# Attention over tokens on one Trainium2 core: the late scores and the late products taken by pairs of images instead of by fours

## The reference

```python
x = x + _L0_conv_ref(_gn(x), ...)       # deformable attention, 16 keys an image
t = _to_tokens(x)                       # 8 images, 256 tokens, 32 channels
t = t + _L1_attn_ref(_ln_t(t))          # below
t = t + _L1_ffn_ref(_ln_t(t), ...)      # 16 experts, each takes its 8 best tokens of an image

def _L1_attn_ref(inputs):
    scores = jnp.einsum('bqd,bkd->bqk', inputs, inputs)
    weights = jax.nn.softmax(scores, axis=-1)
    return jnp.einsum('bqk,bkd->bqd', weights, inputs)
```

## Time and profile before

| | before |
|---|---|
| median of 3 runs | 58.74 us |
| the profiled execution | 58.65 us |
| its span | 56.5 us |
| TensorE busy, share of the span | 48.0 us, 85% |
| VectorE busy | 38.7 us |
| ScalarE busy | 29.3 us |
| granted clock of TensorE | 0.999 |

### The profile page before, as it was taken

How to read it: one execution, slowest core, us unless ns; L and a number is a source line. 1 busy time by engine, 2 the same in 40 slices (tenths; PEclk the granted TensorE clock), 3 DMA queues, 4 the chain that set the end, 5 groups by cost and what they waited for, 6 DMA issues and landing times.

```text
span 56.5 us, 1445 instructions
## 1 busy us (share of the span) xinstructions
PE 48.0 (85%) x568; PEld 38.6 (68%) x568; DVE 38.7 (68%) x102; ACT 29.3 (52%) x68; POOL 20.2 (36%) x48
## 2 busy tenths in 40 slices
PE   3996997799699888999989947979999998979910
PEld 3994795687378776889867925655788585968600
DVE  2459399881849999959998475658368866685440
ACT  0813032696999396004865465297964839801000
POOL 6116389857678889960071040300000000000000
PEclk9999999999999999999999999999999999999999
DMA  0699941110000000000000000000000000000013
GB/s 0 158 194 274 240 158 46 59 46 22 0 0 0 0 0 12 6 0 0 0 0 0 0 0 6 0 0 12 0 0 0 0 0 0 12 0 0 0 49 137
DMA packets 3926, 2.02 MB, mean 36 GB/s; under 512 B 2640, under 2 KB 3792, under 8 KB 3920
## 3 DMA queue, kind: packets, MB, share of 16 engines
q1 hardware_dynamic: 1424, 1.37, 8.8%
q10 hardware_dynamic: 2496, 0.57, 4.7%
HBM read 1.68 MB, written 0.26 MB: 34 GB/s over the span
## 4 chain that ended last, share of the span: by engine, by line
PE 44%; DVE 19%; POOL 15%; ACT 7%; issue 5%; DMA 5%; DVEq 0%; ACTq 0%; POOLq 0%
DMA x_sb<-x_rows 5%; PE ps L711 4%; PE ps L792 4%; PE ps L917 3%; PE ps L858 3%; PE ps L900 3%; PE ps L804 3%; DVE taps L1100 3%; PE ps L922 2%; POOL w_smp L504 2%; ACT e_tok L654 2%; POOL d_prob L412 2%; PE ps L721 2%; DVE off L1102 2%; PE ps L747 2%
## 5 line engine op out<-in xcount | busy, mean ns | idle before, releaser
L711 PE MATMUL ps<-zeros 128*128 128x128 bf16 x128 | 10.8, 246 | 1.0 <-DVE zeros L1081 1.0
L711 PEld LDWEIGHTS ps<-zeros 128*128 128x128 bf16 x128 | 9.5, 113 | 1.5 <-DVE zeros L1081 1.0
L538 ACT ACT_TABLE_LOAD x4 | 5.1, 1283 | 1.7 <-PEq L1326 1.7
L654 ACT ACTIVATE e_tok<-ps,cst 128x512 f32<-128x512 f32 (+1 forms) x6 | 4.5, 828 | 1.5 <-PE ps L900 1.5
L1131 DVE COPY_PREDICATED ps<-over,ps 128x608 f32<-128x608 uint32 (+1 forms) x4 | 3.1, 776 | 0.7 <-PE ps L764 0.7
L453 POOL TENSOR_TENSOR wblk<-wts,cst 128x256 f32<-128x256 f32 x4 | 2.5, 625 | 2.4 <-DMA wts<-weights 2.4
L764 PE MATMUL ps<-rpe_blk,minus_hat_rel 128*32 128x168 f32 x64 | 2.8, 316 | 0.5 <-DVE minus_hat_rel L1127 0.5
L764 PEld LDWEIGHTS ps<-rpe_blk,minus_hat_rel 128*32 128x32 f32 x64 | 2.0, 141 | 1.3 <-issue 0.9
L527 POOL TENSOR_TENSOR x_tok<-ln_c 128x256 f32<-128x256 f32 x2 | 1.2, 617 | 4.7 <-ACT ln_c L639 4.7
L917 PE MATMUL ps<-e_tok,t 128*32 128x128 f32 (+1 forms) x48 | 2.8, 310 | 0.0
L900 PE MATMUL ps<-t_t 32*128 32x256 f32 x32 | 2.3, 398 | 0.4 <-ACT e_tok L654 0.4
(11 more groups left out here) (184 smaller groups left out, 126.8 us busy)
## 6 DMA issues: line engine op xcount, KB each, us to landing
w_sb<-weight ACTq DMA_DIRECT2D x1, 256.0 KB, 6.3
w_sb<-weight SPq DMA_DIRECT2D x1, 256.0 KB, 4.9
x_nat<-x_rows SPq DMA_DIRECT2D x8, 32.0 KB
wts<-weights SPq DMA_DIRECT2D x1, 192.5 KB, 3.9
cst<-shape_consts SPq DMA_DIRECT2D x1, 192.0 KB, 3.5
cst<-shape_consts SPq DMA_DIRECT2D x1, 130.0 KB, 4.8
x_sb<-x_rows SPq DMA_DIRECT2D x1, 128.0 KB, 2.7
x_sb<-x_rows ACTq DMA_DIRECT2D x1, 128.0 KB, 2.8
```

The source lines that it names most:

```text
L538: nc.scalar.add_instruction(mybir.InstLoadActFuncSet(name=nc.get_next_instruction_name(), act_func_set_id=functions, ins=[], outs=[]))
L654: return nc.scalar.activation(dst, scores, ACT.Exp, bias=const("bound"))
L711: mm(bank(n_bank, P), zeros[:, :], zeros[:, :], start=True, stop=True)
```

## The change

Five things are changed together.

1. The second half of tokens is normalised, turned and copied in two pieces, images 0 to 3 and images 4 to 7, each with 128 columns. The pieces are turned into two banks, 7 and 0. The first scores wait for the first piece alone.
2. The turn of the second half of the centred tokens stands behind the scores of images 0 to 3.
3. The scores of the late images are made in two pairs: images 4 and 5 (into banks 4 and 5) after the first exponential, images 6 and 7 (into banks 2 and 3) after the second, with the turn of `x_tok` between them. The banks of the first pair of early images are swapped with it. The fourth exponential now covers images 4 and 5 whole, the last two images 6 and 7 by query half.
4. GpSimd folds images 0 and 1, VectorE images 2 and 3.
5. The products of early and late images go by pair: first both token halves of one pair, then both of the other.

```diff
-        t1t_ps = [bank(6 + h, NT * P).rearrange("p (t m) -> p t m", t=NT) for h in range(NHALF)]
+        t1t_ps = bank(6, NT * P).rearrange("p (t m) -> p t m", t=NT)
+        t1t_late_ps = [bank(n, P) for n in (7, 0)]
-        first_banks, second_banks = [(2, 3), (4, 5)], (6, 7)
-        late_ps = ps[:, 1024:3072].rearrange("p (b h q) -> p b h q", b=B4, h=NHALF)
+        first_banks, second_banks = [(4, 5), (2, 3)], (6, 7)
+        late_ps = [ps[:, 512 * a:512 * a + 1024].rearrange("p (b h q) -> p b h q", b=2, h=NHALF) for a, _ in first_banks]
...
+            pool.wait_ge(exp_ready, NHALF)
+            fold(nc.gpsimd, 0).then_inc(folded_ready, 1)
...
-            act.wait_ge(t1_ready, NHALF)
+            act.wait_ge(t1_ready, 1 + NT)
             keep_centred(1)
...
             act.wait_ge(scores_done, 4)
-            exponent(e_tok[:, B4:, 0], late_ps[:, :, 0]).then_inc(exp_ready, 1)
+            exponent(e_tok[:, B4:B4 + 2], late_ps[0]).then_inc(exp_ready, 1)
+            act.wait_ge(scores_done, 5)
             for q in range(NHALF):
                 queries = slice(P * q, P * q + P)
-                exponent(e_tok[:, B4:, 1, queries], late_ps[:, :, 1, queries]).then_inc(exp_ready, 1)
+                exponent(e_tok[:, B4 + 2:, :, queries], late_ps[1][:, :, :, queries]).then_inc(exp_ready, 1)
...
             keep_busy("t1_second", 5)
-            turn_t1(1)
-            pe.wait_ge(ln_c_ready, 2)
-            turn_half(ct_ps, ln_c, 1).then_inc(c_turned, 1)
+            for t in range(NT):
+                pe.wait_ge(t1_ready, 2 + t)
+                turn_t1(t1t_late_ps[t], 1, t).then_inc(t1_turned, 1)
...
             score_first(0).then_inc(scores_done, 1)
             score_second(0)
+            pe.wait_ge(ln_c_ready, 2)
             score_first(1).then_inc(scores_done, 1)
             score_second(1).then_inc(scores_done, 1)
+            turn_half(ct_ps, ln_c, 1).then_inc(c_turned, 1)
+            pe.wait_ge(t1_copied[1], NT)
+            def score_late(n):
+
+                pe.wait_ge(exp_ready, n + 1)
+                for h in range(NHALF):
+                    for b in range(2):
+                        last = score(late_ps[n][:, b, h], B4 + 2 * n + b, h, start=(h == 0))
+                return last
+
+            score_late(0).then_inc(scores_done, 1)
             for h in range(NHALF):
                 pe.wait_ge(x_tok_ready, h + 1)
                 last = turn_half(conv_ps, x_tok, h)
             last.then_inc(conv_done, 1)
 
+            score_late(1).then_inc(scores_done, 1)
+
             pe.wait_ge(ones_set, 1)
             pe.wait_ge(c_copied, NT)
-            pe.wait_ge(exp_ready, NHALF)
-            for h in range(NHALF):
-                for b in range(B4, B):
-                    last = score(late_ps[:, b - B4, h], b, h, start=(h == 0))
-            last.then_inc(scores_done, 1)
-
-            pe.wait_ge(exp_ready, NHALF + 1)
-            for h in range(NHALF):
-                for b in range(B4):
-                    last = attend(early_ot_ps, b, h, slice(0, M), start=(h == 0), stop=(h == 1))
+            for n in range(2):
+                pe.wait_ge(exp_ready, NHALF + n)
+                for h in range(NHALF):
+                    for b in range(2 * n, 2 * n + 2):
+                        last = attend(early_ot_ps, b, h, slice(0, M), start=(h == 0), stop=(h == 1))
             last.then_inc(ot_done, 1)
...
+            def add_up_late(n, q):
+
+                for h in range(NHALF):
+                    for b in range(B4 + 2 * n, B4 + 2 * n + 2):
+                        last = add_up(late_sums_ps[:, q], b, e_tok[:, b, h, P * q:P * q + P], start=(h == 0), stop=(h == 1))
+                return last
+
+            def attend_late(n, q):
+
+                for h in range(NHALF):
+                    for b in range(B4 + 2 * n, B4 + 2 * n + 2):
+                        last = attend(late_ot_ps[q], b, h, slice(P * q, P * q + P), start=(q == 1 and h == 0), stop=(h == 1))
+                return last
+
             for q in range(NHALF):
-                queries = slice(P * q, P * q + P)
-                for b in range(B4, B):
-                    add_up(late_sums_ps[:, q], b, e_tok[:, b, 0, queries], start=True, stop=False)
-                for b in range(B4, B):
-                    attend(late_ot_ps[q], b, 0, queries, start=(q == 1), stop=False)
+                add_up_late(0, q)
+                attend_late(0, q)
             for q in range(NHALF):
-                queries = slice(P * q, P * q + P)
                 pe.wait_ge(exp_ready, NHALF + 2 + q + 1)
-                for b in range(B4, B):
-                    last = add_up(late_sums_ps[:, q], b, e_tok[:, b, 1, queries], start=False, stop=True)
-                last.then_inc(sums_done, 1)
-                for b in range(B4, B):
-                    last = attend(late_ot_ps[q], b, 1, queries, start=False, stop=True)
-                last.then_inc(ot_done, 1)
+                add_up_late(1, q).then_inc(sums_done, 1)
+                attend_late(1, q).then_inc(ot_done, 1)
...
+            for t in range(NT):
+                images = slice(B4 * t, B4 * t + B4)
+                tt(t1[:, 1, images], centred_ps(1)[:, t],
+                   ln_rstd[:, 0, 1, images].unsqueeze(2).to_broadcast([P, B4, C]), ALU.mult).then_inc(t1_ready, 1)
+
+            for t in range(NT):
+                dve.wait_ge(t1_turned, 2 + t)
+                nc.vector.tensor_copy(t1_t[:, t, P:], t1t_late_ps[t]).then_inc(t1_copied[1], 1)
...
-            for n in range(2):
-                images = slice(2 * n, 2 * n + 2)
-                dve.wait_ge(exp_ready, NHALF + n)
-                tt(e_fold[:, images], e_tok[:, images, 0], e_tok[:, images, 1], ALU.add).then_inc(folded_ready, 1)
+            dve.wait_ge(exp_ready, NHALF + 1)
+            fold(nc.vector, 1).then_inc(folded_ready, 1)
```

More of the change, by code:

```diff
@@ L413, in by_denominator, with fold @@
                                         ALU.mult)
+        def fold(engine, n):
+            images = slice(2 * n, 2 * n + 2)
+            return engine.tensor_tensor(e_fold[:, images], e_tok[:, images, 0], e_tok[:, images, 1], ALU.add)
         @block.sync
@@ L647, in _ @@
             act.wait_ge(t1_turned, 1)
-            nc.scalar.activation(t1_t[:, :, 0:P], t1t_ps[0], ACT.Copy).then_inc(t1_copied[0], 1)
-            act.wait_ge(t1_ready, NHALF)
+            nc.scalar.activation(t1_t[:, :, 0:P], t1t_ps, ACT.Copy).then_inc(t1_copied[0], 1)
+            act.wait_ge(t1_ready, 1 + NT)
             keep_centred(1)
@@ L879, in turn_half, with turn_t1 @@
                 return last
[L881 to L886, removed]
+            def turn_t1(out, h, t):
+                return nc.tensor.transpose(out, t1_rows[:, h, P * t:P * t + P], ident)
             pe.wait_ge(ln_c_ready, 1)
@@ L890, in _ @@
             keep_busy("t1_ready", 5)
-            turn_t1(0)
+            pe.wait_ge(t1_ready, 1)
+            for t in range(NT):
+                last = turn_t1(t1t_ps[:, t], 0, t)
+            last.then_inc(t1_turned, 1)
             keep_busy("t1_second", 5)
-            turn_t1(1)
-            pe.wait_ge(ln_c_ready, 2)
-            turn_half(ct_ps, ln_c, 1).then_inc(c_turned, 1)
+            for t in range(NT):
+                pe.wait_ge(t1_ready, 2 + t)
+                turn_t1(t1t_late_ps[t], 1, t).then_inc(t1_turned, 1)
             def score(scores, b, h, start=True):
@@ L1190, in _ @@
             dve.wait_ge(ln_c_ready, 1)
[L1191 to L1198, removed]
+            dve.wait_ge(ln_rstd_ready, 1)
+            tt(t1[:, 0].rearrange("p (t b) c -> p t b c", t=NT), by_image(ln_c[:, 0]), by_token(ln_rstd[:, 0, 0]),
+               ALU.mult).then_inc(t1_ready, 1)
+            dve.wait_ge(ln_rstd_ready, 2)
+            for t in range(NT):
+                images = slice(B4 * t, B4 * t + B4)
+                tt(t1[:, 1, images], centred_ps(1)[:, t],
+                   ln_rstd[:, 0, 1, images].unsqueeze(2).to_broadcast([P, B4, C]), ALU.mult).then_inc(t1_ready, 1)
+            for t in range(NT):
+                dve.wait_ge(t1_turned, 2 + t)
+                nc.vector.tensor_copy(t1_t[:, t, P:], t1t_late_ps[t]).then_inc(t1_copied[1], 1)
             dve.wait_ge(c_turned, 1)
```

## The result

The changed kernel takes 60.25 us (median of 6 runs, 60.13 to 60.55); the kernel before, run beside it, 58.88 (median of 6). Two of the six executions of the kernel before, 59.99 and 60.38 us, are slow ones, and the ratio leaves them out: it is 1.0263, with an interval of 1.0218 to 1.0308. The profiled execution took 60.14 us with a span of 58.1 us, against 58.65 and 56.5.

The account below looks back on a forecast made before the run. TensorE's queue was taken to bound the kernel; 0.68 + 0 + 1.54 - 0.25 = +1.97 on the profiled 58.65 us gave 60.6 us. The forecast's own range was 60.1 to 61.0, the 8-in-10 range 59.0 to 61.1.

Parts of the forecast that it names:

- Tokens in two pieces: Start of the first scores: 35.18 instead of 35.58 us, -0.40 (bounds -0.25 and -0.50).
- Up to the first product: TensorE from early scores to first product: four scores in two groups cost what eight did, products start at 39.48, +0.68.
- Exponentials and folds at nothing: ScalarE's exponentials and the folds on GpSimd and VectorE: their waits are covered, so they cost nothing.
- Early products by pair: Products of images 0 to 3: three rounds instead of two, sums sharing the third, late products after three as now: 0.
- Late products by pair: Late sums and products: images 6 and 7 begin with the eighth round of 4 and 5, +1.54 (bounds 0 and 1.76).
- starts in program order: TensorE's queue: a matmul doesn't start before the one ahead of it has started; the late products' 1.54 follows this rule.
- a queue that is one matmul deep: Variant for the late products: gains one round, 60.4 us, inside the forecast's range; no chance of its own.
- Behind them: Squares after the late products: query halves end further apart, the 0.22 us wait goes, -0.25 (bounds 0 and -0.35).
- the chances for a change within 2%: Verdict odds: 0.20 from the full-overlap rival, most of the double-rate rival, and 0.03 for terms all too high.
- pairs fully beside each other: Rival for the late products: images 6 and 7 pass 4 and 5, eight rounds as now, 59.1 us; chance 14%.
- no overlap at all: Rival for products and sums: early ones take five rounds, late ones +1.76, +3.08 in all, 61.7 us; chance 5%.
- two groups at double rate: Rival for scores and products: operand stream limits a round, four late scores cost 0.54, 58.0 us; chance 5%.

Follow-up runs that it names:

- r2_together: The changed kernel with the turn of `x_tok` moved ahead of both pairs of late scores, so the pairs stand next to each other: 58.92 us, ratio 1.0046.
- p3_folds: The changed kernel with both folds on VectorE again: 60.3 us, ratio 1.0279.
- r4_by_image: The changed kernel with late sums and products image by image, all eight matmuls of image 4, then 5, 6 and 7: 63.08 us, ratio 1.075.
- s1_scores_by_image: The kernel before with only tokens in two pieces and the later turn of centred tokens, plus late scores image by image: 58.48 us, ratio 0.9963.

## Why the prediction was right, step by step

- **Tokens in two pieces.** Forecast -0.40, measured 35.14 against 35.58, of which 0.05 was there before (the turn of the first half started at 33.94 us instead of 33.99). Right.
- **Up to the first product.** Forecast +0.68, measured +0.62, and block by block: 36.73, 37.80, 38.41 and 39.48 were forecast, 36.71, 37.77, 38.36 and 39.42 came. That four scores in two groups cost what eight in four do is shown, with the addition that the turn between the pairs makes it so (r2_together).
- **Exponentials and folds at nothing.** Right but for 0.07 us: the wait before the fifth is 0.39 us and covered; moving the fold changes nothing (p3_folds). What was missed is that the late sums had waited for the fourth exponential (40.12 us is a round behind the early sums, 40.19 is when they started), and that this wait goes.
- **Early products by pair.** Forecast 0, measured -0.07, which is the wait just named. The 0 is right, but by luck and not for the reason given. They take two rounds as before, not three with the sums in the third: images 2 and 3 pass the second round of 0 and 1, and all four start between 39.42 and 39.64. Either way the late products begin after three rounds.
- **Late products by pair.** This is the term that was mis-sized: +1.54 forecast, +1.29 measured, six more rounds instead of seven (1.31). I had taken starts in program order, which was the wrong mechanism, and had named a queue that is one matmul deep only as a near variant, at one round less. That variant is what runs here. TensorE: Matmul & The Clock Gate in the Trainium skill (Part 3, The mechanism) has matmuls start strictly in program order; the sums at 42.06 ahead of the products at 42.27 contradict it, and r4_by_image measures by how much. TensorEngine Tiling in the Trainium skill (Key Properties) has the tiles independent; in the column groups here that holds for one waiting matmul a group, and no further.
- **Behind them.** Forecast -0.25, measured -0.26; the wait of the earlier trace rows is gone.

The sum was +1.97, and the terms as measured give +1.58; 0.25 of the difference is the one round, 0.07 the wait for the fourth exponential, 0.06 the way to the first product. The right verdict didn't hang on program order: with the queue as it runs the same sum gives 60.4 us. In the chances for a change within 2%, 0.14, 0.04 and 0.03 make 0.21 and not 0.20. The rivals: pairs fully beside each other would have needed a stretch of 1.9 us; no overlap at all is refuted by the early products, 0.89 us as before; two groups at double rate by the score blocks of 1.06 us.

## What to carry to other kernels

Matmuls that used a part of the array ran at full rate here only when the queue brought up all its groups in turn; what mattered is how many went to a group before the others got theirs. Two were free, eight cost six rounds of idle groups, and a full-width matmul between two narrow blocks ended all overlap between them (2.12 us of scores with it, 1.24 without). A busy TensorE doesn't show this: compare the number of records with the length of their stretch (64 in 3.20 us, or in 1.91). And when a step is moved back in a queue, look for an old wait on its result that now stands too early.

## What was not expected of the hardware

Each column group accepts one matmul beyond the one that it runs, so starts can leave program order by that one: in r4_by_image images followed each other at 1.32 to 1.34 us, where eight rounds are 1.75. For row groups at least one is shown (s1_scores_by_image, r2_together). I did not try whether it is one for matmuls of other sizes or types than these fp32 ones of 128 columns (and 256 for the scores and the early products).
